# Gated cross-attention block on one core: the context's probabilities stacked as high, high, low rows by on-chip transfers, with static context keys

## The reference

```
x = x + tanh(g_xattn) * xattn(ctx, layernorm(x))        # x: 2 x 512 x 128, ctx: 2 x 32 x 128
    q = rms(ln @ Wq) * scale;  k, v = split(concat(ctx_n @ Wkv, ln @ Wkv))   # 16 heads of 64
    out = softmax(q k^T, masked over ctx) @ v ; out @ Wout + bout
x = x + tanh(g_ffn) * moe(layernorm(x))                 # 8 experts of 256, top 2 of 8, all computed
```

## Time and profile before

| what | value |
|---|---|
| median of 3 executions | 368.38 us (366.17 to 369.06) |
| the profiled execution | 365.05 us |
| its span | 363.2 us |
| TensorE matmul busy | 313.2 us (86%), 3577 instructions |
| VectorE / GpSimd / ScalarE busy | 287.3 / 256.6 / 195.5 us |

### The profile page before, as it was taken

The page is one execution under the profiler, slowest core; times in us unless marked ns, Lnnn a source line. Parts: engine busy times, 40 slices in busy tenths (PEclk is TensorE's granted clock), DMA queues, the critical chain, the costliest instruction groups (busy, mean ns, idle before and its releaser), DMA issues.

```text
span 363.2 us, 9228 instructions
## 1 busy us (share of the span) xinstructions
PE 313.2 (86%) x3577; PEld 191.8 (53%) x3577; DVE 287.3 (79%) x579; ACT 195.5 (54%) x332; POOL 256.6 (71%) x205
## 2 busy tenths in 40 slices
PE   0654676899999999999999999999996999779993
PEld 0232312356555566555565556787874765336652
DVE  3896678688898898898998976945538988899994
ACT  2555644555656656555656646466663446344651
POOL 8799746698888888987978987456862345245562
PEclk9996786899999999999999999999999999989997
DMA  6407101701602504405207139440000000001000
GB/s 175 125 1 162 21 0 28 155 7 30 153 8 68 116 6 107 79 4 139 50 4 160 26 122 177 124 119 3 2 2 2 0 2 3 1 0 31 3 2 30
DMA packets 31470, 20.38 MB, mean 56 GB/s; under 512 B 11650, under 2 KB 30914, under 8 KB 31426
## 3 DMA queue, kind: packets, MB, share of 16 engines
q1 hardware_dynamic: 30482, 19.75, 23.7%
q10 hardware_dynamic: 944, 0.04, 0.2%
HBM read 5.87 MB, written 0.52 MB: 18 GB/s over the span
## 4 chain that ended last, share of the span: by engine, by line
PE 60%; DVE 14%; issue 11%; POOL 8%; ACT 4%; DMA 1%; POOLq 0%; DVEq 0%
PE big L1344 8%; PE big L1345 7%; POOL p_lo L579 7%; PE big L1234 5%; PE o_ps L1209 5%; PE o_ps L1210 5%; PE o_ps L1215 5%; PE tv L1222 4%; PE pj L1186 3%; DVE nm_main L889 2%; PE pj L1145 2%; PE pj L1147 2%; PE pj L1146 2%; PE tv L1169 1%; PE o_ps L1418 1%
## 5 line engine op out<-in xcount | busy, mean ns | idle before, releaser
L551 POOL TENSOR_TENSOR p_lo<-p 128x1024 f16<-128x1024 f32 x64 | 120.6, 1898 | 20.6 <-ACT p L709 20.4
L709 ACT ACTIVATE p<-big 128x1024 f32<-128x1024 f32 x64 | 65.5, 1024 | 56.9 <-PE big L1345 56.9
L889 DVE TENSOR_REDUCE nm_main<-big 128x2 f32<-128x1024 f32 x64 | 78.3, 1223 | 19.6 <-PE big L1234 19.1
L579 POOL TENSOR_TENSOR p_lo<-p,p_lo 128x512 f16<-128x512 f32 x32 | 37.0, 1158 | 47.1 <-ACT p_lo L774 44.8
L456 POOL TENSOR_TENSOR rms_r<-meansq,power 128x8 f32<-128x8 f32 x32 | 52.2, 1637 | 23.4 <-DVE meansq L864 19.0
L1344 PE MATMUL big<-w 128*128 128x512 f16 x128 | 48.7, 381 | 0.8 <-ACT p L709 0.8
L1345 PE MATMUL big<-w 68*128 68x512 f16 x128 | 48.7, 380 | 0.0
L1209 PEld LDWEIGHTS o_ps<-v,p 128*128 128x128 bf16 x512 | 35.5, 99 | 9.2 <-issue 3.8
L1209 PE MATMUL o_ps<-v,p 128*128 128x65 f16 x512 | 40.3, 193 | 0.0
L1210 PE MATMUL o_ps<-v,p 128*128 128x64 f16 x512 | 40.2, 194 | 0.0
L1210 PEld LDWEIGHTS o_ps<-v,p 128*128 128x128 bf16 x512 | 34.0, 97 | 5.3
(11 more groups left out here) (199 smaller groups left out, 748.7 us busy)
## 6 DMA issues: line engine op xcount, KB each, us to landing
w<-hl SPq DMA_DIRECT2D x64, 128.0 KB, 3.4
w<-hl SPq DMA_DIRECT2D x16, 256.0 KB, 3.7
hl<-n_kernel_gating_EDF_dram SPq DMA_DIRECT2D x1, 1024.0 KB, 6.7
hl<-L_ffn_kernel_up_EDF_dram SPq DMA_DIRECT2D x1, 1024.0 KB, 6.9
o_sb<-in_L_xattn_Wkv_dram SPq DMA_DIRECT2D x2, 384.0 KB, 7.1
x_sb<-in_x_dram SPq DMA_DIRECT2D x2, 256.0 KB, 4.4
wout<-in_L_xattn_Wout_dram SPq DMA_DIRECT2D x1, 512.0 KB, 5.2
k1c<-kc_hl SPq DMA_DIRECT2D x32, 8.0 KB, 2.3
```

What stands on the lines that cost most here:

```text
L551: nc.gpsimd.tensor_tensor(p_lo[m % NP][:, :], p[m % NP][:, :], p_hi[m % NP], ALU.subtract).then_inc(plo_ok, 1)
L579: nc.gpsimd.tensor_tensor(hid_lo[m % NH], hid[m % NH], hid_hi[m % NH], ALU.subtract).then_inc(hlo_ok, 1)
L709: nc.scalar.activation(p[n % NP][:, :], st_ps, ACT.Exp).then_inc(exp_ok, 1)
L889: nc.vector.tensor_reduce(nm_main[:, u % 2, 2 * c:2 * c + 2, q], s2_ps.rearrange("p (k n) -> p k n", k=2), AX_X, ALU.max, negate=True).the ...
```

## The change

- The context's probabilities leave ScalarE twice: `pc_hi` in 16 bits and `pc` in 32 bits. GpSimd forms `pc_lo` from both. SyncE then copies, head by head, the 32 rows of `pc_hi`, the same again, and the 32 rows of `pc_lo` below each other into `pc_st`, 96 rows. `Vst` holds for all heads the matching values (high, low, high), built once. One product of 96 rows by 65 columns stands for three.
- The 12 products of a head's context become 4, and stand after the low parts of the slot rather than before them.
- The context keys `K1c` and `K2c` are built once for all units; the 6 transfers of keys and 4 of values in each unit go. The 4 transfers into `W2` become 2 of twice the size (the row blocks of `W2` change places). The queue gets 12 transfers of 32 KB in each unit.
- The context scores move in slot 8u from the end to right after `score`, ScalarE's two exponentials stand in slot 8u (after the slot's own exponential), and `pc_lo` in slot 8u + 1.
- Some clearing of buffers at the start goes, and a clearing of `Vst` comes.

```diff
-        K1c = [sb(f"k1c{k}", [P, 640], F16) for k in range(2)]
-        K2c = [sb(f"k2c{k}", [P, 640], F16) for k in range(2)]
-        Vbd = [sb(f"vbd{k}", [P, HG, VW], F16) for k in range(2)]
+        K1c = sb("k1c", [P, H // 2, 2, BC], F16)
+        K2c = sb("k2c", [M_ROWS, H // 2, 2, BC], F16)
+        Vst = sb("vst", [3 * C, B, H, DH + 1], F16)
...
+            def stack(u, h):
+                for k, part in enumerate((pc_hi, pc_hi, pc_lo)):
+                    if h == 0 and k == 2:
+                        sp.wait_ge(cplo_ok, u + 1)
+                    sp.dma_start(pc_st[u % 2][C * k:C * (k + 1), h, :], part[C * h:C * (h + 1), :]).then_inc(pcst_ok[h], 16)
+
             def slot(n):
+                if n - 1 in cst_at:
+                    u = cst_at[n - 1]
+                    need(sp, pv_ok, 8 * (u - 1))
+                    sp.wait_ge(cexp_ok, u + 1)
+                    for h in range(HG):
+                        stack(u, h)
                 if n in W_AT:
...
-                        sp.dma_start(w2[0:DH, 0:2, odd, :], hl[rows, 1, 0:2, :]).then_inc(w2_ok[u % 2], 16)
-                        sp.dma_start(w2[0:DH, 2:4, odd, :], hl[rows, 0, 2:4, :]).then_inc(w2_ok[u % 2], 16)
+                        sp.dma_start(w2[0:DH, :, odd, :], hl[rows, :, :, :].rearrange("p a c n -> p (a c) n")[:, 2:6, :]
+                                     ).then_inc(w2_ok[u % 2], 16)
...
-                if n - 2 in cst_at:
-                    u = cst_at[n - 2]
+                if n - 1 in cst_at:
+                    u = cst_at[n - 1]
                     pool.wait_ge(cexp_ok, u + 1)
...
+                    nc.gpsimd.tensor_tensor(pc_lo[:, :], pc[:, :], pc_hi[:, :], ALU.subtract).then_inc(cplo_ok, 1)
...
-                if n - 1 in cst_at:
-                    u = cst_at[n - 1]
+                if n in cst_at:
+                    u = cst_at[n]
                     act.wait_ge(cst_ok, u + 1)
...
+                    nc.scalar.activation(pc_hi[:, :], o_ps[0][:, :], ACT.Exp, bias=mask_c[:, batch(u):batch(u) + 1])
+                    nc.scalar.activation(pc[:, :], o_ps[0][:, :], ACT.Exp,
                                          bias=mask_c[:, batch(u):batch(u) + 1]).then_inc(cexp_ok, 1)
                 if n in t_at:
                     high_halves(t_at[n])
...
-                    values(o_of, pc_hi[u % 2], slice(0, 512), v[:, 0:DH + 1], v[:, DH + 1:VW], False)
-                    values_lo(o_of, pc_lo[u % 2], slice(0, 512), v[:, 0:DH + 1])
                 pe.wait_ge(plo_ok, m + 1)
...
+                    pe.wait_ge(pcst_ok[h], 48 * (u + 1))
+                    last = values_lo(o_of, pc_st[u % 2][:, h, :], slice(0, 512), Vst[:, batch(u), HG * group(u) + h, :])
                 last.then_inc(pv_ok, 1)
```

More of the change, by code:

```diff
@@ L132, in flamingo_gated_block @@
         p_lo = [sb(f"p_lo{k}", [P, 1024], F16) for k in range(NP)]
-        pc = [sb(f"pc{k}", [P, 512], F32) for k in range(2)]
-        pc_hi = [pc[k][:, :].bitcast(BF16).rearrange("p (n two) -> p n two", two=2)[:, :, 1] for k in range(2)]
-        pc_lo = [sb(f"pc_lo{k}", [P, 512], F16) for k in range(2)]
+        pc = sb("pc", [P, 512], F32)
+        pc_hi = sb("pc_hi", [P, 512], F16)
+        pc_lo = sb("pc_lo", [P, 512], F16)
+        pc_st = [sb(f"pc_st{k}", [3 * C, HG, 512], F16) for k in range(2)]
         inv = sb("inv", [P, 2, QT], F32)
@@ L196, in flamingo_gated_block @@
         out_ok = sem("out_ok")
+        pcst_ok = [sem(f"pcst_ok{h}") for h in range(HG)]
         kc2_z, kc2_ok = sem("kc2_z"), sem("kc2_ok")
@@ L381, in slot @@
+                if n == FIRST:
+                    sp.wait_ge(cklo_ok, 1)
                     for odd in range(2):
                         rows = slice(DH * odd, DH * (odd + 1))
[L383 to L397, removed]
+                        for k, part in ((K1c[0:DH], 0), (K1c[DH:P], 1), (K2c[0:DH], 0)):
+                            sp.dma_start(k[:, :, odd, :], kc_hl[rows, part, :, :]).then_inc(kc_ok, 16)
@@ L398, in slot @@
+                if n == -1:
+                    sp.wait_ge(const_z, 4)
+                    sp.wait_ge(cvlo_ok, 1)
+                    for b in range(B):
+                        for k, cols in enumerate((slice(0, DH + 1), slice(DH + 1, VW), slice(0, DH + 1))):
+                            sp.dma_start(Vst[C * k:C * (k + 1), b, :, 0:cols.stop - cols.start],
+                                         vc[b * C:(b + 1) * C, :, cols]).then_inc(vbd_ok, 16)
                 if n - 1 in nm_at:
@@ L439, in _ @@
             for part in (lnT_hi, lnT_lo):
-                nc.gpsimd.memset(part[:, B * N + BC:LNW], 0.0)
+                last = nc.gpsimd.memset(part[:, B * N + BC:LNW], 0.0)
+            last.then_inc(const_z, 1)
             def rsqrt(c):
@@ L479, in _ @@
             rsqrt(CH_B0B)
-            for k in range(2):
-                nc.gpsimd.memset(K1c[k][:, :], 0.0)
             nc.gpsimd.memset(kc2[:, :, :, :, :], 0.0).then_inc(kc2_z, 1)
@@ L485, in _ @@
             weights_lo(0)
-            for k in range(2):
-                nc.gpsimd.memset(Vbd[k][:, :, :], 0.0).then_inc(const_z, 1)
+            nc.gpsimd.memset(Vst[:, :, :, :], 0.0).then_inc(const_z, 1)
             pool.wait_ge(lnlo_ok, 2)
@@ L1350, in slot @@
                     score(j)
+                if n in cst_at:
+                    u = cst_at[n]
+                    if u:
+                        pe.wait_ge(o_ok, HG * (u - 1) + 3)
+                    else:
+                        pe.wait_ge(nmc_ok, 1)
+                    if u == 0:
+                        pe.wait_ge(kc_ok, 96)
+                    for w, k, rows, q in ((W1, K1c, P, 0), (W2, K2c, M_ROWS, 2)):
+                        for h in range(HG):
+                            last = nc.tensor.matmul(o_ps[0][C * h:C * (h + 1), :], k[0:rows, 2 * group(u) + h // 2, h % 2, batch(u) * C:(batch(u) + 1) * C],
+                                                    w[u % 2][0:rows, q + h // 2, h % 2, :], start=(w is W1), stop=(w is W2))
+                    last.then_inc(cst_ok, 1)
                 if n in t_at:
@@ L1407, in slot @@
                     last.then_inc(nmT_ok, 1)
-                if n in cst_at:
-                    u = cst_at[n]
-                    if u:
-                        pe.wait_ge(o_ok, HG * (u - 1) + 3)
-                    else:
-                        pe.wait_ge(nmc_ok, 1)
-                    pe.wait_ge(kc_ok[u % 2], 96 * (u // 2 + 1))
-                    for w, k, rows in ((W1, K1c, P), (W2, K2c, M_ROWS)):
-                        for h in range(HG):
-                            last = nc.tensor.matmul(o_ps[0][C * h:C * (h + 1), :], k[u % 2][0:rows, 160 * h:160 * h + C],
-                                                    w[u % 2][0:rows, h // 2, h % 2, :], start=(w is W1), stop=(w is W2))
-                    last.then_inc(cst_ok, 1)
                 if n - 1 in TURN_AT:
```

63 lines of the change are left out of this document (24 added, 39 removed).

## The result

The changed kernel takes 372.75 us (median of 4 runs, 371.69 to 374.11). The kernel before took 367.27 us (median of 4 runs, 364.75 to 369.06). The ratio is 1.017, with a 95% interval of 1.013 to 1.022: slower, by 5.5 us in the medians. The profiled executions stand further apart: 374.11 us (span 372.3) against 365.05 (span 363.2), 9.1 us.

A forecast was written before the change was run, and what follows sets the result against it. TensorE was taken as the middle's bound, two chains within half a microsecond. Slots 0 to 8 -0.5, units +0.9, +3.5, +1.2, from slot 48 -1.0: +4.1 us, 369.1 profiled, 372.4 as median, range 363.5 to 379.

The forecast's parts named there:

- (d): The forecast itself: early scores delay each unit more than removed products save; 369.5 to 376 us, chance 0.60.
- The early scores: Slot 8u: context scores wait half a microsecond for their bank, two exponentials delay the squares; turn in slot 26 waits 0.9.
- first pass: Unit times before the bank's further 0.24 us delay: squares at 4.29, power at 6.11, turn in slot 26 at 8.59.
- GpSimd between the powers: GpSimd's two `p_lo` and `pc_lo` keep their length, 4.7 us, so the next power starts at 12.41 instead of 10.98.
- So TensorE is the bound in the middle: Middle units: TensorE, busy 24.95 of 25 us and nearly gapless, sets the 25.7 us unit.
- the round trip: A q and k tile's way from projection through squares, power and scaling to its turn; slack about 0.4 us.
- rival (a): Only TensorE's work counts, so the removed products come off in full: -7.8 us, 360.6; chance 0.15.
- Weight loading as headroom: Skill's rule: weight loading busy 14.90 of 25 us leaves TensorE far from full; removed products buy nothing, sum 4 us higher.
- No wait on `pcst_ok`: The first head's stack lands at 12.9 us in the unit, TensorE asks at about 13.5, so it never waits.
- rival (c): Stack copies queue behind the weights and land at 16.2 us in the unit: +13 more, 385; chance 0.08.
- After slot 48: Slots 53 and 55 give 0.5 us, slot 56 loses 0.7 at the bank, slots 57 to 65 give 1.2: together -1.0.
- The start: The removed and added clearing of buffers lie beside GpSimd's waits: 0, with 0.2 us either way.

The follow-up runs named there:

- early_only: Kernel before with only the context scores moved up behind `score` in slot 8u and their one exponential into slot 8u; 372.49 us, 1.0158 of before.
- late_scores: Changed kernel with the context scores back at the end of slot 8u and both exponentials back in slot 8u+1; 364.78 us, 0.9944 of before.
- exps_last: Changed kernel with ScalarE's two context exponentials placed behind the evacuation and the squares in their slot; 370.74 us, 1.0101 of before.
- pc_lo_first: Changed kernel with VectorE's low part of the values ahead of the scaling, and GpSimd's `pc_lo` ahead of the power; 365.13 us, 0.9959 of before.
- swap_after: Changed kernel with VectorE forming the low part of the values before the q/k tile's scaling; 368.37 us, 1.0058 of before.
- four_products: Kernel before without the eight products per head using the context probabilities' high half, output wrong by that part, nothing moved; 363.69 us, 0.9924 of before.
- swap_late: Changed kernel with context scores and exponentials back in their late places, and VectorE's low part of the values before the scaling; 360.91 us, 0.9852 of before.
- stack_first: swap_late with SyncE issuing unit 6's stack copies ahead of unit 7's weights; 368.24 us, 1.0049 of before.
- swap_four: four_products with VectorE's low part of the values before the scaling; 360.24 us, 0.9838 of before.
- double_stack: swap_late with 20 stack copies of 32 KB per unit instead of 12, the product waiting for all of its head; 369.24 us, 1.0059 of before.

## Why the prediction came out as it did

**The total** was forecast at 372.4 (+4.1 on before in the profiled execution) and measured at 372.75 (+5.5 in the medians). That the total came so near is luck in part: the increase was 1.4 us larger than forecast, and the kernel before, measured with a fourth execution, had a median 1.1 us lower (367.27) than the 368.38 that the forecast added to. The mechanism is the forecast's, (d). Its terms hold to different degrees. Of the profiles' 9.1 us, 7.1 lie behind slot 0, where 4.1 was forecast: of the missing 3.0, the units from slot 8 to 48 hold 1.5 and the time after slot 48 the other 1.5.

**The early scores: right, almost to the hundredth.** From slot 8u on the steady-state forecast had everything 0.24 later than its first pass. Scores at 2.04 (measured 2.04), evacuation at 3.88 (3.86), squares at 4.53 (4.47), power at 6.35 (6.32), turn in slot 26 at 8.83 (8.83) with a wait of 0.9 (0.85). early_only shows the cause alone: 1.0 us per unit. In the changed kernel late_scores and exps_last part it: 0.58 for the exponentials ahead of the squares, 0.97 for the rest of the early place, above all TensorE's with the bank's wait.

**GpSimd between the powers: undersized.** The forecast let 6.30 us pass from power to power; it is 158.76 - 152.18 = 6.58. I had taken 4.7 us for the three subtractions, where the rows of before already had 152.47 - 147.62 = 4.85; the rest, 0.13, is `pc_lo`, which takes 1.16 instead of 1.04. It now reads `pc_hi` from a tile of its own; whether that is the reason, no run shows. So what stands between the two powers is not quite the same work as before. That is the whole of the unit's error, 1.43 against 1.16 (turn in slot 28 at 16.07, forecast 15.81). pc_lo_first shows that this chain decides slot 28: with 1.16 us out of it the wait of 0.56 that swap_after had there goes.

**"So TensorE is the bound in the middle": the step that failed.** The forecast gave the round trip a slack of 0.4 us and priced a product of slots 29 and 31 in full. four_products has 0.24 us per unit for 0.97 removed, 2.55 us in all instead of rival (a)'s 7.8. The start-to-start rows showed no gap but 0.27, and yet at slot 28 the chain had no slack at all: of the 0.5 saved in slots 25 and 27 it took all back, and of the 0.5 of slots 29 and 31 it took half back in slot 24. In the changed kernel this did no harm to the forecast, since there the savings of slots 25 and 27 were written off anyway, and those of slots 29 and 31 were set against a later bank. It would have made any forecast of late_scores wrong: mine for that kernel was 25.0, measured 25.58.

**Weight loading as headroom.** The rule of the Trainium skill ("Perfetto Trace Analysis", Identifying the Most-Contended Engine) had the removed products buy nothing, and my starts had them count. With the chain as it is, the rule came nearer (0.24 of 0.97). With the chain shortened the same products count for 0.74, and TensorE is all but packed (0.23 us of waiting in a unit of swap_late) at a weight loading of 14.39 in 25 us. Neither busy row said it; the swap did.

**No wait on `pcst_ok`: right in the middle units, wrong in unit 6.** There slots 48 to 50 turn no tile, TensorE asks for the stack 10.9 us after the unit's start instead of 13.4. And the first head's last copy is issued 7.7 us after it, close behind the unit's 1.5 MB of weights, instead of 11.0, when these have long been issued:

```profile
237.43 0.30 PE L1221 MATMUL o_ps<-vst,pc_st 96*128 96x65 f16 x4 [0.98 <-DMA pc_st<-pc_lo]
...
256.08 0.40 PE L1367 MATMUL o_ps<-w,k1c 128*32 128x512 f16 x4 [1.45 <-DVE o_sb L1057]
```

This is rival (c)'s mechanism, which had a chance of 0.08, in the one unit in which I had not looked for it: 4.1 us from issue to landing where I had taken 2. stack_first confirms the queue behind the weights: the copy is issued as late as in swap_late (7.2 and 7.3 us into the unit), but with no weights ahead of it lands in 3.0 us instead of 4.7 and is in time.

**After slot 48: -1.0 forecast, +0.5 measured** (0.12 + 0.97 - 0.48 - 0.08). Slots 48 to 55 should have gained 0.5 and lost 0.12. The stack's wait made slot 51 0.91 longer, but slot 52 was 0.74 shorter. The larger loss is 0.77 in slot 54: ScalarE waits 1.41 us for the down-projection's weights, issued 15.8 us into unit 6 against 11.2 before, and TensorE 0.61 behind it. The row of after:

```profile
248.85 0.62 ACT L761 CAST wd_hi<-v 128x512 f16<-128x512 f32 x1 [1.41 <-DMA v<-ffn_kernel_down_EFD_dram]
```

Slot 56 lost 0.97 instead of 0.7 (a wait of 1.45 for the bank). Slots 57 to 65 gave 0.56 of 1.2: slots 57 and 59 by 0.24 each, and from slot 61 on other work ends last.

**The start: 0 within 0.2 forecast, +1.97 in the profile, and most likely not the change's.** late_scores, exps_last and the changed kernel are the same up to slot 0, and it starts at 63.97, 61.06 and 63.08; before it is 61.11, in four_products 61.74 and in early_only 62.59. Over all traces, slot 0 starts at 62.2 on average both in the five kernels with the old start and in the eight with the new. The traces part at TensorE's first projections, which differ in when they speed up. In the changed kernel's profile:

```profile
16.29 0.63 PE L1151 MATMUL big<-wqkv_hl,lnT_hi 128*128 128x512 f16 x1
16.71 0.63 PE L1152 MATMUL big<-wqkv_hl,lnT_hi 128*128 128x512 bf16 x1
...
18.85 0.42 PE L1151 MATMUL tv<-wqkv_hl,lnT_hi 128*128 128x256 f16 x1
19.06 0.34 PE L1152 MATMUL tv<-wqkv_hl,lnT_hi 128*128 128x256 bf16 x1
19.24 0.27 PE L1153 MATMUL tv<-wqkv_hl,lnT_lo 128*128 128x256 f16 x1
19.35 0.27 PE L1151 MATMUL tv<-wqkv_hl,lnT_hi 128*128 128x256 f16 x1
```

and in that of exps_last:

```profile
16.33 0.56 PE L1151 MATMUL big<-wqkv_hl,lnT_hi 128*128 128x512 f16 x1
16.73 0.38 PE L1152 MATMUL big<-wqkv_hl,lnT_hi 128*128 128x512 bf16 x1
16.95 0.38 PE L1153 MATMUL big<-wqkv_hl,lnT_lo 128*128 128x512 f16 x1
```

So 2 of the 9.1 us between the profiles are no more than two runs of one program differ by at this point. That leaves 7.1, the medians say 5.5, and their interval (1.3% to 2.2%, 4.7 to 7.9 us) holds both.

## What to carry to other kernels

An engine without gaps is only a bound if the next chain is far behind it; before pricing work that is removed from it, measure the next chain's slack at each place where the two meet, or leave the work out once and look. Work that many others wait for (here a bank, then squares, power, scaling) is moved ahead only if its input is ready there: 0.55 us of products moved half a slot forward cost 1.0 us per unit in early_only and 1.55 in the changed kernel, more than 256 fewer products could give. Where an engine idles before one step and has another ready for the same waiter, swap them: here two blocks of VectorE's code exchanged gave 0.9 us per unit with the late scores and the stack, and brought that kernel 1.5% below the one before.

## What the runs showed of the hardware

**When TensorE speeds up differs from run to run.** 512 columns took 0.43 us from start to start, then 0.21, the levels of 1.2 and 2.4 GHz by these rows, in every trace; the step came between 16.7 and 19.2 us, at other times in programs that are the same up to there (16.7 in exps_last, 17.5 in late_scores, 19.1 in the changed kernel). The granted clock in the profile reads 1.00 in these stretches both before and after the step, so here it was the distance of the starts that told. The Trainium skill ("TensorE: Matmul & The Clock Gate", What's actually happening) calls the point of the step variable from run to run; these traces agree, but their spread of 2.5 us is wider than the 0.5 us to either side that the section gives. The step isn't all that varies (late_scores starts slot 0 later than the changed kernel, with an earlier step), and what else does stays open; by slot 0 the same program was up to 2.9 us apart.

**A small VectorE operation can last until GpSimd's beside it ends.** The mean square (128 x 8) takes 0.17 us, but 1.10 in slot 27 of the changed kernel, from 157.57 to 158.67, up to the end of GpSimd's `p_lo` (156.76 to 158.65). In swap_late it takes 0.76 there and ends at 150.58, `p_lo` at 150.55. The row of after:

```profile
157.57 1.10 DVE L870 TENSOR_SCALAR meansq<-sumsq 128x8 f32<-128x8 f32 x1
```

The Trainium skill ("SBUF — State Buffer", SBUF: two separate sides) tells of one pair of ports that VectorE in some modes and GpSimd hold for a whole instruction; the end of the one at the end of the other agrees with it. No run here prices it alone, since the power that follows had to wait for `p_lo` anyway.

**Copies of 32 KB on the chip** took 0.6 us each on SyncE's queue and 1.8 to 1.9 from issue to landing with nothing ahead, 4.1 (changed kernel) and 4.7 (swap_late) behind weights. As long as TensorE did not wait for them, they cost a unit nothing measurable: the 0.12 us between swap_late and swap_four are GpSimd's `pc_lo`, and the unit from slot 24 lasts 24.69 with twelve copies (swap_late) and with twenty (double_stack); what they cost is their place in the queue.
